# Softmax sums from halved exponentials: key halves added on GpSimd and VectorE ahead of the ones product, and four output buffers

## The reference

```python
x = x + tanh(g_xattn[0]) * mha(layernorm(x), ctx, ctx, ...)
x = x + tanh(g_ffn[0]) * ffn(layernorm(x), ...)
# mha, for each head:
scores = einsum('bhqd,bhkd->bhqk', q, k) / sqrt(dk)
p = softmax(scores, axis=-1)
o = einsum('bhqk,bhkd->bhqd', p, v)
```

## Time and profile before

| | |
|---|---|
| median of 3 runs | 1876.81 us (1875.94 to 1877.08) |
| profiled execution | 1879.23 us, span 1877.1 us |
| TensorE busy | 1650.6 us, 88% |
| VectorE busy | 1335.6 us, 71% |
| ScalarE busy | 813.3 us, 43% |
| GpSimd busy | 519.0 us, 28% |
| mean granted TensorE clock | 0.947 |

### The profile page before, as it was taken

The page is one execution under the profiler, slowest core; times in us unless marked ns, Lnnn a source line. Parts: engine busy times, 40 slices in busy tenths (PEclk is TensorE's granted clock), DMA queues, the critical chain, the costliest instruction groups (busy, mean ns, idle before and its releaser), DMA issues.

```text
span 1877.1 us, 34921 instructions
## 1 busy us (share of the span) xinstructions
PE 1650.6 (88%) x11820; PEld 778.9 (41%) x11868; DVE 1335.6 (71%) x2109; ACT 813.3 (43%) x1068; POOL 519.0 (28%) x782
## 2 busy tenths in 40 slices
PE   2759989999999899989999999986599999989787
PEld 2324444444344344444444434433344444434333
DVE  6627686686767768758678677676787778878565
ACT  2223524325144152342432514325777777756342
POOL 6213414225233242332422423112000000007644
PEclk7979999999999899989999999999699999999899
DMA  6445554454444544545445544325244553015997
GB/s 191 124 119 113 130 150 112 120 126 132 127 111 125 138 116 130 116 117 137 125 124 117 147 124 93 98 57 203 90 168 169 191 214 144 23 45 228 343 415 300
DMA packets 271526, 274.48 MB, mean 146 GB/s; under 512 B 156721, under 2 KB 205873, under 8 KB 268849
## 3 DMA queue, kind: packets, MB, share of 16 engines
q1 hardware_dynamic: 271408, 272.73, 48.5%
HBM read 126.10 MB, written 62.39 MB: 100 GB/s over the span
## 4 chain that ended last, share of the span: by engine, by line
issue 59%; POOL 12%; PE 11%; DVE 7%; DMA 5%; SPq 3%; POOLq 1%; ACT 1%; DVEq 0%; ACTq 0%
DMA x<-out_dram 4%; POOL ol L549 3%; POOL yh L604 3%; PE bank L1274 3%; PE bank L1175 2%; POOL xres L556 2%; PE bank L1176 2%; PE bank L1177 2%; SPq L362 2%; DVE mx L891 2%; POOLq L263 1%; POOL nw L531 1%; PE spair L1256 1%; POOL nw L529 1%; POOL nw L533 1%
## 5 line engine op out<-in xcount | busy, mean ns | idle before, releaser
L643 ACT ACTIVATE pr<-spair 128x1024 f32<-128x1024 f32 x256 | 258.9, 1019 | 96.6 <-PE spair L1256 96.5
L891 DVE TENSOR_REDUCE mx<-spair 128x4 f32<-128x1024 f32 x256 | 300.2, 1214 | 0.4 <-PE spair L1231 0.4
L636 ACT ACTIVATE parts<-bank,bqk 128x512 f16<-128x512 f32 x128 | 87.9, 687 | 302.8 <-PE bank L1177 302.8
L864 DVE SCALAR_TENSOR_TENSOR parts<-bank,bqk,parts 128x512 f16<-128x512 f32 x128 | 95.2, 749 | 162.4 <-ACT parts L636 162.4
L1371 PE MATMUL spair<-xqT,wgT 128*128 128x512 bf16 x684 | 179.6, 382 | 2.6 <-ACT xqT L751 1.6
L1371 PE MATMUL spair<-xqT,wuT 128*128 128x512 bf16 x691 | 180.1, 381 | 0.7
L1274 PE MATMUL bank<-pr,v 128*32 128x256 f32 x2048 | 143.4, 399 | 32.5 <-DVE o L885 32.4
L1256 PE MATMUL spair<-stacks 128*128 128x256 f16 x1024 | 155.0, 279 | 8.1 <-DMA stacks<-mT 7.7
L1175 PE MATMUL bank<-xT,wqT 128*128 128x512 f16 x256 | 104.2, 407 | 62.7 <-issue 28.7
L734 ACT ACTIVATE sil<-spair,gsc 128x512 f32<-128x512 f32 x176 | 118.2, 680 | 75.5 <-PE spair L1371 75.5
L657 ACT ACTIVATE mT<-bank 64x128 f16<-64x128 f32 x16 | 4.3, 269 | 337.4 <-PE bank L1240 337.4
(11 more groups left out here) (162 smaller groups left out, 3227.6 us busy)
## 6 DMA issues: line engine op xcount, KB each, us to landing
stacks<-parts SPq DMA_DIRECT2D x768, 64.0 KB, 2.0
x<-out_dram SPq DMA_DIRECT2D x32, 1024.0 KB, 11.2
h_spill<-hb SPq DMA_DIRECT2D x10, 2816.0 KB, 9.2
hb<-h_spill SPq DMA_DIRECT2D x10, 2816.0 KB, 15.3
xbuf<-in_x_dram SPq DMA_DIRECT2D x16, 1024.0 KB, 5.4
cbuf<-in_ctx_dram SPq DMA_DIRECT2D x16, 1024.0 KB, 5.9
xres<-in_x_dram SPq DMA_DIRECT2D x16, 1024.0 KB, 5.2
out_dram<-xres SPq DMA_DIRECT2D x16, 1024.0 KB, 4.8
```

The costliest lines, as they stand in the source:

```text
L643: act.activation(pr[:, u % 4, :, :, :].rearrange("p a b q -> p (a b q)"), spair[u % 2][:, :, :].rearrange("p a q -> p (a q)"), ACT.Exp, sc ...
L891: dve.tensor_reduce(mx[:, h:h + 2, b, :], spair[u % 2][:, :, :].rearrange("p a (q k) -> p a q k", q=KH), AX_X, ALU.max).then_inc(max_done, 1)
```

## The change

Before the ones product, the two key halves of the exponentials are added: for the first pair of heads of a step on GpSimd (`add_even`), for the second on VectorE (`add_odd`), into `ph`, which has one buffer. The ones product then reads `ph` in four matmuls instead of eight. Both adds wait until the step before has used `ph` (`pv_mm`). `o32` gets four buffers, and `norm(g)` waits for step g - 4. On GpSimd `o_low` moves a step later, and the four `residual` tiles move from the start of the body to steps 4 to 7.

```diff
-        o32 = alloc(p1, "o32", [P, 2, S], F32)
+        o32 = alloc(p1, "o32", [P, 4, S], F32)
+        ph = alloc(p1, "ph", [P, 2, 2, S], F32)
...
+            def add_even(j, g):
+
+                wait(pool, exp_done, j * NU + 2 * g + 1)
+                wait(pool, pv_mm, j * NGR + g + 2)
+                pool.tensor_tensor(ph[:, 0, :, :], pr[:, (2 * g) % 4, :, 0, :], pr[:, (2 * g) % 4, :, 1, :],
+                                   ALU.add).then_inc(even_added, 1)
...
-            def residual(j):
+            def residual(j, t):
 
                 wait(pool, res_in, j * 16 + 16)
-                for t in range(NT):
-                    pool.tensor_tensor(xres[:, t, :], xres[:, t, :], tgbo[:, :], ALU.add).then_inc(res_bias, 1)
+                pool.tensor_tensor(xres[:, t, :], xres[:, t, :], tgbo[:, :], ALU.add).then_inc(res_bias, 1)
...
             def body(j, nxt):
-                residual(j)
                 for g in range(NGR):
+                    add_even(j, g)
                     if nxt is not None:
                         if g < NT:
                             low_c(nxt, g)
                         else:
                             low_x(nxt, g - NT)
-                    if g > 0:
-                        o_low(j, g - 1)
+                    if g > 1:
+                        o_low(j, g - 2)
                     if g == 2 and nxt is not None:
                         x_rstds(nxt)
+                    if g >= NT:
+                        residual(j, g - NT)
+                o_low(j, NGR - 2)
                 o_low(j, NGR - 1)
                 x1_rstds(j)
...
+            def add_odd(j, g):
+
+                wait(dve, exp_done, j * NU + 2 * g + 2)
+                wait(dve, pv_mm, j * NGR + g + 2)
+                dve.tensor_tensor(ph[:, 1, :, :], pr[:, (2 * g + 1) % 4, :, 0, :], pr[:, (2 * g + 1) % 4, :, 1, :],
+                                  ALU.add).then_inc(odd_added, 1)
+
             def norm(j, g):
                 wait(dve, pv_mm, j * NGR + g + 1 + 2)
-                if g >= 2:
-                    wait(dve, o_hi, j * NGR + g - 1)
-                    wait(dve, o_lo, j * NGR + g - 1)
+                if g >= 4:
+                    wait(dve, o_hi, j * NGR + g - 3)
+                    wait(dve, o_lo, j * NGR + g - 3)
...
                 for g in range(NGR - 1):
+                    add_odd(j, g)
                     norm(j, g)
...
-                for ones in (False, True):
-                    for kh in range(KH):
-                        for a in range(HPC):
-                            h = HPC * c + a
-                            at = S if ones else 0
-                            last = pe.matmul(obank[DK * a:DK * a + DK, at:at + S],
-                                             onesP[:, :] if ones else v[:, 2 * b + kh, DK * h:DK * h + DK],
-                                             pr[:, (2 * g + a // 2) % 4, a % 2, kh, :],
-                                             start=(kh == 0), stop=(kh == KH - 1))
+                for kh in range(KH):
+                    for a in range(HPC):
+                        h = HPC * c + a
+                        pe.matmul(obank[DK * a:DK * a + DK, 0:S], v[:, 2 * b + kh, DK * h:DK * h + DK],
+                                  pr[:, (2 * g + a // 2) % 4, a % 2, kh, :], start=(kh == 0), stop=(kh == KH - 1))
+                wait(pe, even_added, j * NGR + g + 1)
+                wait(pe, odd_added, j * NGR + g + 1)
+                for a in range(HPC):
+                    last = pe.matmul(obank[DK * a:DK * a + DK, S:2 * S], onesP[:, :],
+                                     ph[:, a // 2, a % 2, :], start=True, stop=True)
                 last.then_inc(pv_mm, 1)
```

More of the change, by code:

```diff
@@ L188, in gated_block_kernel @@
         exp_done = sem("exp_done")
+        even_added = sem("even_added")
+        odd_added = sem("odd_added")
         pv_mm = sem("pv_mm")
@@ L548, in o_low @@
                 wait(pool, v_mm, j * NT + NT)
-                pool.tensor_tensor(ol[:, c, b * S:b * S + S], o32[:, g % 2, :], oh[:, c, b * S:b * S + S],
+                pool.tensor_tensor(ol[:, c, b * S:b * S + S], o32[:, g % 4, :], oh[:, c, b * S:b * S + S],
                                    ALU.subtract).then_inc(o_lo, 1)
-            def residual(j):
+            def residual(j, t):
                 wait(pool, res_in, j * 16 + 16)
-                for t in range(NT):
-                    pool.tensor_tensor(xres[:, t, :], xres[:, t, :], tgbo[:, :], ALU.add).then_inc(res_bias, 1)
+                pool.tensor_tensor(xres[:, t, :], xres[:, t, :], tgbo[:, :], ALU.add).then_inc(res_bias, 1)
             def x1_rstds(j):
@@ L651, in o_high @@
                 wait(act, v_mm, j * NT + NT)
-                act.activation(oh[:, c, b * S:b * S + S], o32[:, g % 2, :], ACT.Copy).then_inc(o_hi, 1)
+                act.activation(oh[:, c, b * S:b * S + S], o32[:, g % 4, :], ACT.Copy).then_inc(o_hi, 1)
             def mT_copy(i):
@@ L884, in norm @@
                 wait(dve, recip_spread, j * NGR + g + 1)
-                dve.tensor_tensor(o32[:, g % 2, :], obank[:, 0:S], rs[:, g % 2, :], ALU.mult).then_inc(norm_done, 1)
+                dve.tensor_tensor(o32[:, g % 4, :], obank[:, 0:S], rs[:, g % 2, :], ALU.mult).then_inc(norm_done, 1)
             def key_max(i, u):
@@ L986, in body @@
                     key_max(i, 1)
+                add_odd(j, NGR - 1)
                 norm(j, NGR - 1)
```

## The result

The changed kernel took 2494.0 us (median of 4 runs, 2491.5 to 2496.4) against 1876.9 us before: a ratio of 1.3285, with a 95% interval of 1.325 to 1.3321. The forecast was 2440 us, the range 2255 to 2540.

A forecast was written before the change was run, and what follows sets the result against it. TensorE, 88% busy, was taken to bound the kernel at 5.43 us a step. Fourteen full groups at 26.8 us plus 12.7 for the clock gave 553 us, the last two 10: 2440 us, range 2255 to 2540.

The forecast's parts named there:

- The ring through GpSimd: Attention step: next ones product waits for GpSimd's add, queued behind work needing this step's projection; 7.9 us instead of 5.43.
- O(1) and O(2): Ones products of steps 1 and 2 in a group: released by GpSimd's add, +2.1 and +2.4 us.
- the clash: GpSimd and VectorE hold each other up at SBUF: 0.15 us per step, +1 us a group.
- the top of a group: Step 0's ones product waits for VectorE's add behind two `qk_low`: mean +2.5 us over fourteen groups.
- the clock: TensorE's granted clock falls after idle waits, slowing the work behind them: 12.7 us a full group.
- The steps: Distances between successive ones products in a full group, from step 0 to step 7, longest into step 3: 12.1 us.
- The rival's 0.45 us in each of 98 steps: VectorE's add and GpSimd's work exclude each other fully: 44 us more, about 2485 us; chance 12%.
- a long wait: TensorE idling before a ones product in the four long cases of a group: 2.0 us clock loss each.
- The two short waits: TensorE idling 2.6 to 2.9 us before the ones products of steps 1 and 2: 1.2 us clock loss each.
- the one before O(0): TensorE's wait before step 0's ones product: 2.0 us clock loss in 8 of 14 groups.
- V(1): Value product of step 1: in the kernel before, waits 0.7 us for the normalization in 8 groups.
- The last two groups: Groups with no x or context tile to prepare, so GpSimd's add is early: 10 us together.

The follow-up runs named there:

- e1: Changed kernel with GpSimd's add of step g+1 moved ahead of the low half of step g; 2202.9 us.
- e3: Changed kernel with both adds moved early in their queues; 1915.5 us, ratio 1.0225 to the kernel before.
- e4: Changed kernel with GpSimd's four residual tiles moved behind step 7; 2447.3 us.
- e5: Changed kernel with each value product issued four times over, to keep TensorE busy while it waits; 2385.5 us.
- e2: Changed kernel with VectorE's add moved right behind the normalization, GpSimd's left in place; 2421.6 us.
- e7: Changed kernel with GpSimd's add alone, in its place; the second pair enters the ones product as two halves, without VectorE's add; 2321.8 us.
- e9: Changed kernel with both adds early, only in steps 1, 2, 3, 5 and 6; 1843.0 us, ratio 0.981 to the kernel before.
- e10: Changed kernel with VectorE's add alone, early, in steps 1 to 6, no GpSimd add; 1866.5 us, ratio 0.9936 to the kernel before.

## Why the prediction was right, point by point

- **The ring through GpSimd** was right and is shown by e1, e3 and e4: undoing the order, not the adds, takes away 578 of 617 us. Its stations in steps 3 to 7 are those of the text. That the total came out so near is in part luck: the waits of O(1) and O(2), the clash and the top of a group were priced too low, the clock too high.
- **The steps.** Forecast without the clock: 7.6, 7.9, 12.1, 8.5, 9.8, 9.8, 7.6. At the full clock (e5) the distances were 8.3, 8.9, 12.4, 10.3 into O(5), 10.3 into O(6) and 7.9 into O(7); so these terms were 0.3 to 1.0 too low. The one into O(4) was 10.4 to 12.0 even there, since TensorE still idles 4.6 us ahead of O(3) in that run; without a clock loss its rows add up to about 9.1, an estimate. All seven together were 3.8 us too low, of which 1 was set aside for the clash.
- **O(1) and O(2)** were a miss of mechanism: VectorE's add releases them, not GpSimd's. The x tile statistics of these steps (1.28 us) and the moments stand ahead of it, which I left out of VectorE's sum, and the add itself takes 1.71 us there, beside GpSimd's `ph`:

```profile
370.75 1.28 DVE L849 BATCH_NORM_STATS2 bst<-xbuf 128x6 f32<-128x512 f32 x2
...
371.84 1.26 POOL L551 TENSOR_TENSOR ph<-pr 128x512 f32<-128x512 f32 x1
371.94 1.71 DVE L888 TENSOR_TENSOR ph<-pr 128x512 f32<-128x512 f32 x1
```

  It costs 0.7 and 1.0 us a group, some 24 us in all: with VectorE's add moved away (e2) the same two distances are 7.6 and 7.8 at the full clock, which is GpSimd's ring as forecast.
- **The clash** was mis-sized: I put 0.15 us a step. In the rows of step 3 to step 4 `cl` has 1.31 to the next instruction instead of 1.16, which I had, and `ol` 1.07 instead of 0.65, which I hadn't: 0.6 us. VectorE's add shows 1.64 us instead of 0.68 and ends at 407.05, 0.54 after `cl` (406.51), as if most of it began only then; `ol` ends 0.5 after that. The Trainium skill (SBUF — State Buffer, "Who interferes with whom") says that a VectorE instruction with two SBUF inputs contends with a GpSimd one that reads SBUF, and calls the contention an exclusive lock; the trace agrees. The rival's 0.45 us in each of 98 steps is the size in the steps into O(4) to O(6), 0.35 (`cl`) into O(3) and 0.46 (GpSimd's `ph`) into O(7); in steps 1 and 2 it is VectorE that waits. Its total of about 2485 was nearer than my forecast in number. But in e2 and e7, in which `ol` is back at 0.67 us, the steps into O(4) to O(6) are hardly shorter, so the clash alone doesn't explain the 54 us.
- **The clock.** I took 2.0 us for a long wait. From the ones product at 398.27 to V at 403.90 it is 5.63 us; at the full clock it would be 0.55 (e9) and 3.57 (606.13 to 609.70): 1.5 us. Against e5 the distances into O(5), O(6) and O(7) are 1.3, 2.3 and 0.8 us longer, so the mean of the four is 1.5: too high by 0.5 in four steps. The two short waits cost 1.4 and 1.6 us instead of 1.2, the one before O(0) less than its term. The mean of 14 groups for the seven steps came out at about 77 us, against 76 forecast: the clock, too dear, hid most of what the steps had too cheap.
- **The top of a group** was under-priced. From O(7) to the next O(0) it takes 41.1 to 41.9 us, before 34.8 to 42.9, mean 37.7: 3.8 more, where my terms gave 2.3. Part of the reason can be read in one group: GpSimd's `ph` of step 0, which was free to run there now, meets VectorE's four `ndev` tiles:

```profile
356.64 2.87 DVE L934 TENSOR_SCALAR ndev<-xres,mv,r 128x512 f32<-128x512 f32 x4 [3.72 <-POOL r L542]
...
356.82 1.50 POOL L551 TENSOR_TENSOR ph<-pr 128x512 f32<-128x512 f32 x1 [0.21 <-issue]
...
361.85 1.40 DVE L876 SCALAR_TENSOR_TENSOR parts<-bank,bqk,parts 128x512 f16<-128x512 f32 x2
363.16 0.68 DVE L888 TENSOR_TENSOR ph<-pr 128x512 f32<-128x512 f32 x1
363.99 1.08 PE L1298 MATMUL bank<-ph,onesP 128*32 128x256 f32 x8 [5.20 <-DVE ph L888]
```

The tiles take 2.87 us here and 1.91 in other groups. But the top is 41.6 us on the mean in the groups with 2.87 and 41.3 in those with 1.91, so this is only a small part; what makes up the rest of the 1.5 us stays open. My count was off as well: `qk_low` comes behind O(0) in 7 of the 14 full groups, not in 8. The eighth, with the row at 1192.57 in the earlier trace rows, belongs to the fifteenth group. That makes the term 0.2 us smaller. V(1) waited in 6 of them, not 8.

- **VectorE's add** took 0.68 us undisturbed (0.6 forecast), but 1.21 on the mean of all 128; GpSimd's took 1.26 (1.27).
- **The sum.** From O(0) of the first group to that of the fifteenth it was 1065.5 us and is 1658.9: 42.4 us a group, 39.5 forecast. The last two groups cost about 21 us more, 10 forecast. Together that is 51 of the 54 us by which 2440 fell short; the other 3 lie before the first O(0) and behind the last ones product.

## What to carry to other kernels

Before work goes to a half idle engine, look at what stands ahead of it in that engine's fixed order, and what that waits for: here adds on engines that were busy for 28% and 71% of the time made 617 us of loss, because each stood behind work that waited for the step's own projection. Place such an add where its inputs are ready and its reader is near, and leave it out where the queue can't deliver it in time. And when a set of matmuls in separate strips is to be cut down, see that every strip gets shorter: cutting two strips of four gave nothing here.

## What the runs showed of the hardware that was not expected

- A VectorE tensor_tensor with both inputs in SBUF and GpSimd's tensor_tensor hold each other up: 1.64 us instead of 0.68 for the one, 1.07 instead of 0.65 for the other. VectorE's tensor_scalar on one float32 tile in SBUF took 1.38 us instead of 0.54 beside GpSimd's add (e1).
- Six matmuls in four strips of 32 rows cost 0.97 us (e10), about as eight do (0.98); four, one in each strip, cost 0.55 (e9).
- TensorE, kept busy with three useless copies of a product while it waited, made the kernel 108 us faster (granted clock 0.83 to 0.95).
